# Feed-forward of the first five batches dealt over six batches of the attention layer instead of five

## What is computed

```python
xn = _rms_norm(x, g_norm) * (1.0 + scale) + shift
qkv = xn @ W_qkv
q = _rms_norm(q, g_q)
k = _rms_norm(k, g_k)
logits = jnp.einsum('bhqd,bhkd->bhqk', q, k) * d ** (-0.5)
attn = jax.nn.softmax(logits, axis=-1)
o = jnp.einsum('bhqk,bhkd->bhqd', attn, v)
return o + o @ W_out
...
y1 = x1 @ w_up + b_up + x1 @ w_up_lora_a @ w_up_lora_b
x2 = jax.nn.relu(y1)
y2 = x2 @ w_down + b_down + x2 @ w_down_lora_a @ w_down_lora_b
```

## Time and profile before

| | us |
|---|---|
| median of 3 runs | 2815.45 |
| lowest and highest run | 2814.27, 2816.41 |
| profiled execution | 2816.0 |
| its span in the trace | 2814.3 |
| third batch (192.4 to 266.0) | 73.6 |
| fourth batch | 92.7 |
| fifth, sixth, seventh batch | 91.9, 89.9, 90.8 |
| eighth batch | 89.2 |

### The profile page before, as it was taken

One profiled execution on the slowest core, in us unless ns is written; L12 is line 12 of the kernel. 1 busy time (PEld: TensorE's weight loads), 2 busy tenths in 40 slices (PEclk: granted clock), 3 DMA queues, 4 the chain that ended last, 5 costly groups with the idle time before them and its releaser, 6 DMA issues.

```text
span 2814.3 us, 133061 instructions
## 1 busy us (share of the span) xinstructions
PE 2691.5 (96%) x49384; PEld 2406.8 (86%) x49384; DVE 1781.3 (63%) x6337; ACT 1132.4 (40%) x4965; POOL 1340.6 (48%) x3458
## 2 busy tenths in 40 slices
PE   7887999999899899999999999999999999999998
PEld 5555777877799899999989998998999899899987
DVE  5877856666555466666666666666666666666654
ACT  3543465556244333333333333333333333333322
POOL 1210022112366666666656665665666566566500
PEclk8988999999999899999999999999999999999999
DMA  6543555445200034444334443433443434444476
GB/s 195 182 127 126 161 164 173 144 159 171 81 4 4 3 118 127 130 135 129 126 117 139 130 128 124 129 126 125 132 129 119 130 128 130 127 130 127 128 237 196
DMA packets 140076, 365.06 MB, mean 130 GB/s; under 512 B 17584, under 2 KB 27440, under 8 KB 139184
## 3 DMA queue, kind: packets, MB, share of 16 engines
q1 hardware_dynamic: 137328, 355.88, 39.9%
q10 hardware_dynamic: 2560, 6.49, 0.7%
HBM read 327.83 MB, written 34.47 MB: 129 GB/s over the span
## 4 chain that ended last, share of the span: by engine, by line
PE 69%; DVE 2%; issue 2%; DMA 0%; ACT 0%; DVEq 0%; POOL 0%; ACTq 0%; SPq 0%; POOLq 0%
PE pscan L1559 14%; PE pscan L1555 14%; PE pg L1461 12%; PE pd L1512 12%; PE pu L1461 12%; PE pd L1485 2%; PE pg L1473 1%; PE pu L1473 1%; PE prouter L1473 1%; PE prouter L1573 0%; PE prouter L1581 0%; DVE state L1688 0%; DMA wgu<-w_split 0%; ACT th L1368 0%; PE pd L1588 0%
## 5 line engine op out<-in xcount | busy, mean ns | idle before, releaser
L1555 PEld LDWEIGHTS pscan<-th,carry 128*128 128x128 f16 x16384 | 560.0, 96 | 38.9 <-ACT th L1368 17.8
L1555 PE MATMUL pscan<-th,carry 128*128 128x8 f16 x16384 | 559.6, 166 | 14.3 <-ACT th L1368 14.1
L1559 PE MATMUL pscan<-th,carry 128*128 128x16 f16 x16384 | 558.8, 169 | 3.3 <-DVE th L1671 2.3
L1559 PEld LDWEIGHTS pscan<-th,carry 128*128 128x128 f16 x16384 | 482.7, 96 | 5.2 <-DVE th L1671 4.6
L1368 ACT ACTIVATE th<-state 128x32 f16<-128x32 f32 x768 | 176.0, 229 | 707.9 <-DVE state L1688 707.7
L1461 PE MATMUL pg<-qh,wgu 128*128 128x256 f16 x3168 | 430.1, 275 | 16.0 <-issue 15.2
L1512 PE MATMUL pd<-hg,wd 128*128 128x256 f16 x3168 | 430.9, 275 | 2.2 <-DMA wd<-w_split 2.2
L1461 PE MATMUL pu<-qh,wgu 128*128 128x256 f16 x3168 | 427.0, 274 | 0.0
L1688 DVE TENSOR_REDUCE state<-pscan 128x32 f32<-128x96 f32 x768 | 197.9, 258 | 282.7 <-PE pscan L1559 279.2
L1461 PEld LDWEIGHTS pg<-qh,wgu 128*128 128x128 f16 x3168 | 295.3, 98 | 54.9 <-issue 16.6
L1461 PEld LDWEIGHTS pu<-qh,wgu 128*128 128x128 f16 x3168 | 294.6, 98 | 34.0
(11 more groups left out here) (256 smaller groups left out, 4697.3 us busy)
## 6 DMA issues: line engine op xcount, KB each, us to landing
wgu<-w_split SPq DMA_DIRECT2D x264, 512.0 KB, 3.5
wd<-w_split SPq DMA_DIRECT2D x264, 384.0 KB, 3.1
parts_mem<-in_w_tiles SPq DMA_DIRECT2D x159, 256.0 KB, 3.5
w_split<-parts_mem SPq DMA_DIRECT2D x99, 256.0 KB, 2.7
late<-in_w_tiles SPq DMA_DIRECT2D x39, 256.0 KB, 3.9
w_split<-late SPq DMA_DIRECT2D x33, 128.0 KB, 3.0
hid<-in_up_q SPq DMA_DIRECT2D x8, 512.0 KB, 4.0
hid<-in_up_s SPq DMA_DIRECT2D x16, 256.0 KB, 5.0
```

The lines of the kernel that those rows point to most:

```text
L1555: mm(pscan[:, 0, m * B:(m + 1) * B], clo[:, k, m * P:(m + 1) * P], th[:, k, 0, :], start=(m == 0 and k == 0), stop=False, skip_group_check ...
L1559: ins = mm(pscan[:, 0:2, m * B:(m + 1) * B], chi[:, k, m * P:(m + 1) * P], th[:, k], start=False, stop=(k == NC - 1), skip_group_check=True)
```

## The change

A table of slots replaces the fixed lists. It runs over the third to the eighth batch (`FFN_FROM = 2`) and deals the 160 parts of the five batches in one sequence, so that a batch's slots hold the end of one feed-forward and the start of the next: 26 parts in the third, 27 in each of the fourth to seventh, 26 in the eighth. In detail the projection slots hold 0, 1, 1, 2 in the third batch and 1, 1, 1, 2 in the others; the first quad 3, 1, 1, 1, 1; the second and third 1 in each slot; the fourth 1, 1, 1, 0, 1; the last slot 1, but none in the eighth.

```diff
-        ffn_qk = [[0], [1], [2, 3], [4, 5]]
-        ffn_quad = [[[6, 7, 8], [9], [10], [11], [12, 13]], [[14, 15], [16], [17], [18], [19]],
-                    [[20, 21], [22], [23], [24], [25]], [[26, 27], [28], [29], [], [30]]]
-        ffn_last = [31]
+        FFN_FROM, BLOCKS = 2, HC + 4 * NC
+        LAST = NC + 5 * NC
+        def slot_of(c, g):
+            return NC + 5 * c + g
+        ffn_slots, at = {}, 0
+        for b in range(FFN_FROM, B):
+            sizes = [b > FFN_FROM, 1, 1, 2] + [3, 1, 1, 1, 1] + 2 * [1, 1, 1, 1, 1] + [1, 1, 1, 0, 1] + [b < B - 1]
+            for slot, size in enumerate(sizes):
+                ffn_slots[b, slot] = [divmod(at + i, BLOCKS) for i in range(size)]
+                at += size
...
+        def blocks(b, *slots):
+            return [block for slot in slots for block in ffn_slots.get((b, slot), [])]
...
-                ffn = b >= LAG
-                def relus(parts):
-                    for part in parts:
-                        if ffn and part < HC and part % 2:
-                            relu(b - LAG, part // 2)
+                ffn = b >= FFN_FROM
+                def relus(*slots):
+                    for n, part in blocks(b, *slots):
+                        if part < HC and part % 2:
+                            relu(n, part // 2)
+                        if part == 5:
+                            act.wait_ge(S["d_x2"], 2 * n + 2)
+                            act.dma_start(x_old, dram["x"][:, n]).then_inc(S["x_again"], 16)
...
-                if ffn:
-                    n = b - LAG
-                    act.wait_ge(S["d_x2"], 2 * n + 2)
-                    act.dma_start(x_old, dram["x"][:, n]).then_inc(S["x_again"], 16)
...
+                relus(LAST)
...
+                    if (b, c) == (FFN_FROM, 1):
+                        pe.wait_ge(S["split"], PIECES - 2)
+                        pe.wait_ge(S["split_end"], 2)
+                    for n, part in blocks(b, c):
+                        ffn_part(n, part)
...
-            for b in range(LAG):
-                batch(b, False, True)
-            with pe.Fori(LAG, B - 1) as b:
-                batch(b, True, True)
-            batch(B - 1, True, False)
+            for b in range(B):
+                batch(b, b >= FFN_FROM, b + 1 < B)
...
+            ended = []
+            def lows(b, *slots):
+                while ended:
+                    second(*ended.pop(0))
+                for n, part in blocks(b, *slots):
+                    if part < HC and part % 2:
+                        hidden_low(n, part // 2)
+                    if part in (HC + 2 * NC - 1, BLOCKS - 1):
+                        ended.append((n, part // (BLOCKS - 1)))
```

70 lines of the change are left out of this document (33 added, 37 removed).

## The result

| | us |
|---|---|
| kernel before, median (7 runs beside the changed one) | 2815.92 |
| changed kernel, median of 7 runs | 2824.76 |
| lowest and highest | 2823.03, 2828.05 |
| ratio | 1.0033, 95% interval 1.0024 to 1.0042 |
| its profiled execution, span | 2823.0 |

The changed kernel is slower by 8.8 us; the forecast was 10 us faster. In the two profiles the attention layer is 13.1 us longer (the scan's first matmul stands at 763.0 us, before at 749.9). The first two batches, which the change leaves alone, took 1.7 us more here, and the stretch from the eighth batch to the scan 1.7 less. Everything from the scan on was 4.4 us shorter in this execution, which is no gain: over all traces of this study that unchanged stretch took 2060 to 2067 us.

What follows compares the result with a forecast made beforehand. PE, busy for 96% of the span, was taken as the bound, with DVE nearly the chain in the fourth batch. 9.8 + 1.2 - 6.0 - 5.9 - 5.4 - 3.8 = -10.1 us gave 2805.3 us, range 2793 to 2811.

Steps and rivals of the forecast that it cites:

- PE's price of a part: A feed-forward part is 12 matmuls on PE; the next group starts 1.31 us after the part's first one.
- Third batch: Gains 26 parts: PE's floor 80.5 us at full clock plus 2.9 us net of waits, 83.4 us, +9.8.
- Fourth batch: Loses 5 parts, 6.6 us on PE, but DVE is nearly the chain in attention: +1.2 us, between -6.6 and +4.
- part 2 behind the write-back: Fourth batch's first quad: part 2 waits for DVE's write-back of part 31's bank, starting at 299.8 instead of 298.58.
- (a): One part less between the projections earns 0.3 of 1.31 us, as stores hold the first transposes; eighth 0 to 0.2.
- (b): First quad, fifth to seventh batch: one part less, down parts needing no remainder, saves 3.0, 2.6 and 2.8 us.
- (c), (d): Heads of second and third quads, fifth to seventh batch: one part less saves 1.3 us each, about 0.7 less beside rectifiers.
- (e): Fourth quad, fifth to seventh batch: one part less, 1.31 us less lost cover, gives 0.6 to 1.2 us back.
- Eighth: Loses 6 parts, with nothing saved in the first quad: -3.8 us, between -1 and -7.9.
- the wait for part 14: Eighth batch's first quad: part 14 needs the remainder of parts 10 and 11, not there before 668.3; nothing saved.
- Moved at no cost: Input reload moved to part 5's slot, mostly covered by three heads, and PE's loop made straight code: 0 us.
- the covers were gone: Rival, chance 0.10: each of the last five batches gives back only 1.5 to 3 us, total 2813 to 2818 us.

Runs made afterwards that it cites:

- e6: Changed kernel, copies and remainders of the second layer's weight parts moved behind the eighth batch: fifth to eighth batch 335.9 us, against 358.8 with them.
- e14: Changed kernel, no part in the third batch but the order of a batch with parts, 32 parts in the others: third batch 77.5 us.
- e7: Changed kernel with one copy of a weight part in each projection slot of the fifth to eighth batch instead of three: ratio 1.0105 to the kernel before.
- e10: Changed kernel with every store of a weight part's halves cut to an eighth of one half: fifth to eighth batch 351.7 us, against 358.8.
- e13: Changed kernel, 16 parts in third and eighth batch, 32 between, down parts 16 to 31 before next up parts: fifth to seventh batch 94.2 to 96.8 us.
- e3: Changed kernel with each quad's fourth row maximum moved directly behind the other three on VectorE: 2820.69 us, ratio 1.0016 to the kernel before.
- e9: Changed kernel with copies and remainders of weight parts cut to 64 of 512 columns: fifth to eighth batch 340.6 us, against 358.8.
- e15: Changed kernel, four parts in the third batch's projection slots, its attention in the old order, 31 parts in four batches: ratio 1.0064 to the kernel before.
- e1: Kernel before with only the PE loop over the fourth to seventh batch written out as straight code: 2817.62 against 2816.49 us, ratio 1.0009.
- e5: Kernel before, copies and remainders of the second layer's weight parts moved behind the eighth batch: fifth to eighth batch 352.2 us, against 361.6 with them.
- e2: Changed kernel with all 32 parts one batch earlier, none in the eighth: eighth batch 84.1 us, ratio 1.0065 to the kernel before.

## Why the prediction was wrong, point by point

- **PE's price of a part, 1.31 us:** right. With full clock and no preparation the batches show 81 to 82 us of PE (e6), as worked out.
- **Third batch, +9.8:** +12.0 in the two profiles, +14 against the 71 us that four of six traces of the old third batch show. PE's 80.5 us and the clock of 1.0 were right, and no wait was over 2 us: the query wait was 1.2, the first transposes 0.6, a remainder 0.6, the fourth quad 1.4. The net of waits was 5.1 us instead of 2.9; 1.3 of the 2.2 missing is the wait for the norm behind part 15's rectifier, which the prediction did not book. Luck entered by the base: the 73.6 us came with a lower clock than four of the others. That the order of a batch with parts has a price of its own, 5 to 6 us of waiting (e14), was nowhere in the sum; PE's floor hides most of it.
- **Fourth batch, +1.2:** +4.0 in this profile, +0.7 in five others of the same fourth batch, so right. The mechanism was right too, part 2 behind the write-back; its wait was 2.48 us in all of them. The other 3.2 us are half clock behind the waits (granted clock 0.90 and 0.82 in the first and the fourth quad, against 1.00 and 0.90 in e7).
- **(a) The projection part, 0.3:** gave 0.9 to 1.3, and 2.3 in the eighth. The stores did hold back the first transposes, at 30.8 to 33.9 us instead of the 30.8 that all four batches have without preparation; with small stores (e10) they came at 30.8 to 32.0.
- **(b) First quad, 3.0, 2.6, 2.8:** 2.5 and 2.5 in the fifth and the sixth; in the seventh, with down parts too, 1.0 lost, since the first transposes came at 33.9 us, with 2.51 us of waiting.
- **(c), (d):** forecast 2.0, 1.9 and 2.6; got 0.3, 1.7 and 2.6. Right in two. In the fifth the missing 1.7 is mostly the 1.31 us for the norm behind part 5's rectifier.
- **(e) The fourth quad, +0.7 to +1.1 given back:** the step that failed. It cost 2.7, 5.7 and 2.6 us. I counted one part less, and took the kind of the others for unimportant; 11.0 us lost where 2.6 were booked. e13 shows that the kind decides, e3 that a little under half of it is the row maximum's place, and e6 and e9 that it takes the weight parts' copies and remainders beside them: without these it is 4.1 us. e10 rules out the stores there.
- **Eighth, -3.8:** -1.6. The wait for part 14 was foreseen, at "nothing saved". The next scores came 1.3 us later in the batch than before: the projection gave 2.3 and the first quad took 3.6. The 1.3 is what the part behind the wait took more at half clock (2.74 us instead of 1.47).
- **Moved at no cost:** right for this table, where part 5 falls behind the first quads: no copy on ACT waits for GpSimd's third copy. With part 5 in the projection slots the reload does block ACT (e15). The straight code shows no price (e1).
- **Which rival:** the covers were gone, and the time came out 7 us above that rival's 2813 to 2818, since it had no place that loses. The rows [2] had ACT at 55 us and DVE at 58 of 90, which looks free, and is not, because in attention each head is a chain over DVE, ACT and PE. e5 and e6 would have told it.

The sum of the misses is 2.2 + 2.8 + 4.7 + 6.1 + 5.5 + 2.2 = 23.5 us, and the table's 13.4 less the forecast -10.1 is the same. The whole executions differ by 8.8 us only, since the unchanged stretch behind the layer was 4.4 us shorter in this one.

## What to carry to other kernels

An engine that is busy for 96% can still be only just longer than a chain across the others: before work is taken off it, look for what stretch would be left with the work gone, by a kernel that leaves out what the others do beside it (e5 and e6), or at least by adding up the chain of one head. A kernel that takes all work off the engine itself (e2) also changes its clock, and tells less. Dealing unlike pieces of work evenly changes which piece stands where; a piece with a successor on two other engines is dearer beside the places where those engines are tight, and count alone does not price it. What a place loses changes with the part that stands there, so each place needs its own row, with its own kind of part. Where the profile names no releaser of a wait, the code's own waits at that line do: here an instruction of the next batch. And a table that moves one thing moves what hangs on it, as the reload hangs on part 5.

## What the runs showed of the hardware

After waits of some 2.4 to 3.1 us PE often went on at half clock for up to 3 to 4 us, and not always. The wait of 2.48 us in the fourth batch is the same in eight traces: behind it the changed kernel and e3 lost 1.7 us in that quad (granted clock 0.90), and the six others nothing (1.00 in e7 and e9). In the sixth batch of the changed kernel, ahead of the wait, in it, right behind it, and later (columns as in the earlier trace rows; the clock is the third number from the end):

```profile
537.00:539.50 2.50, 1.57 (x14) 1.07 (x11) 2.50 (x6) 2.46 (x7) 2.50 (x3) 1.00 0.28 104
539.60:542.70 3.10, 0.00 (x1) 0.01 (x1) 3.10 (x6) 1.08 (x5) 1.53 (x2) 1.00 0.25 76
543.20:546.60 3.40, 3.40 (x31) 2.36 (x32) 2.24 (x5) 0.81 (x3) 0.00 (x0) 0.52 0.79 245
547.70:549.10 1.40, 1.40 (x15) 1.03 (x12) 1.15 (x2) 0.81 (x2) 0.00 (x0) 1.00 1.00 362
```

0.52 is the lower of the two levels, 1.2 GHz. It costs 1.2 us on the part (2.55 to the next group instead of 1.31) and 0.4 on the broadcast (1.08 instead of 0.64), so a wait of 3.1 us takes nearly 5 from PE, while waits of 1.18 cost themselves alone. My forecast had the clock at 1.0 throughout; the averages of 0.95 to 0.98 in the fourth to eighth batch are these short spells, and make the 1.6 to 3 us by which PE's busy time exceeds its work. The Trainium skill, "TensorE: Matmul & The Clock Gate", Part 1, says that an idle engine falls back to the lower clock; the trace agrees, for the waits behind which it fell.

The same instructions take different times, mostly by the clock: the third batch of the old order lasted 70.9 to 75.3 us in six traces, the granted clock 0.90 to 0.82, with DVE busy for 55.8 to 56.0 us in each, and PE for 55.1 to 60.3.
